# An image tower on one core: the opening rewritten so that tiles 0 to 3 share one norm and step one takes in two tiles

## What is computed

```python
h = patches(x) @ W                                   # 12544 tokens x 768 -> 256
n = layernorm(h)
x_proj = n @ in_w + in_b
mod = gelu(n @ mod_w1 + mod_b1) @ mod_w2 + mod_b2     # 256 -> 1024 -> 256
y = irfft(rfft(x_proj * mod) * rfft(kernel))          # along the 196 tokens of an image
h = h + y @ out_w + out_b
h = h + ffn(layernorm(h))                             # base, shared, and top 2 of 6 routed experts
```

## Time and profile before

| | us |
|---|---|
| three runs: median, lowest, highest | 1251.4, 1250.5, 1251.81 |
| the profiled execution | 1251.14 |
| its span, from the first to the last instruction in the trace | 1249.4 |
| TensorE busy in the span | 1226.5 (98%) |
| VectorE, ScalarE, GpSimd busy | 861.1, 587.9, 404.2 |
| TensorE's first product starts at | 7.63 |
| first projection (step one) starts at | 30.06 |
| first projection of step two starts at | 58.29 |

### The profile page before, as it was taken

The page is one execution under the profiler, slowest core; times in us unless marked ns, Lnnn a source line. Parts: engine busy times, 40 slices in busy tenths (PEclk is TensorE's granted clock), DMA queues, the critical chain, the costliest instruction groups (busy, mean ns, idle before and its releaser), DMA issues.

```text
span 1249.4 us, 21119 instructions
## 1 busy us (share of the span) xinstructions
PE 1226.5 (98%) x8163; PEld 1200.4 (96%) x8163; DVE 861.1 (69%) x2557; ACT 587.9 (47%) x1110; POOL 404.2 (32%) x463
## 2 busy tenths in 40 slices
PE   5999999999999999999999999999999999999997
PEld 5999999999999999999999999999999999999986
DVE  6467676677666677666677666677666677666676
ACT  5644454444454444454444444444444444444432
POOL 4622332322332322332322332322332322332310
PEclk9999999999999999999999999999999999999999
DMA  7111111011111011111011111011111011110001
GB/s 244 39 39 52 51 48 42 16 49 52 51 44 46 14 51 51 52 42 48 14 52 51 52 39 51 14 52 51 52 39 51 14 52 51 52 39 16 14 13 34
DMA packets 23470, 57.26 MB, mean 46 GB/s; under 512 B 2825, under 2 KB 18506, under 8 KB 19402
## 3 DMA queue, kind: packets, MB, share of 16 engines
q1 hardware_dynamic: 22554, 55.13, 12.7%
q10 hardware_dynamic: 816, 0.79, 0.2%
HBM read 43.07 MB, written 12.85 MB: 45 GB/s over the span
## 4 chain that ended last, share of the span: by engine, by line
PE 95%; DVE 3%; ACT 1%; POOL 0%; DMA 0%; issue 0%; DVEq 0%; POOLq 0%
PE rotating L1237 17%; PE rotating L1239 17%; PE rotating L1238 17%; PE rows_ps L1237 10%; PE rows_ps L1238 10%; PE rows_ps L1239 10%; PE turn L1480 5%; PE turn L1464 2%; PE turn L1276 2%; PE rows_ps L1285 2%; PE turn L1237 1%; PE turn L1238 1%; PE turn L1239 1%; PE rotating L1345 1%; POOL w_l L434 0%; DMA prod<-dram_tok_w 0%
## 5 line engine op out<-in xcount | busy, mean ns | idle before, releaser
L575 ACT ACTIVATE gelu<-rotating,biases 128x392 f32<-128x392 f32 x256 | 149.1, 583 | 203.6 <-PE rotating L1239 203.5
L468 POOL TENSOR_TENSOR folded<-modulated 128x196 f32<-128x196 f32 x63 | 38.1, 604 | 558.0 <-DVE modulated L979 558.0
L455 POOL TENSOR_TENSOR gelu_l<-gelu,gelu_h 128x784 fp32r<-128x784 f32 x62 | 117.4, 1894 | 223.4 <-DVE norm L962 197.4
L440 POOL TENSOR_TENSOR patches_l<-patches,patches_h 128x384 fp32r<-128x384 f32 x186 | 184.8, 1023 | 0.3 <-ACT patches_h L533 0.3
L1237 PE MATMUL rotating<-gelu_h,w_h 128*128 128x392 f32 x512 | 177.7, 347 | 0.0
L1237 PE MATMUL rotating<-x_h,w_h 128*128 128x392 f32 x512 | 177.2, 346 | 0.0
L1239 PE MATMUL rotating<-x_h,w_l 128*128 128x392 f32 x512 | 174.7, 341 | 0.0
L1238 PE MATMUL rotating<-x_l,w_h 128*128 128x392 f32 x512 | 174.6, 341 | 0.0
L1238 PE MATMUL rotating<-gelu_l,w_h 128*128 128x392 f32 x512 | 174.3, 340 | 0.0
L1239 PE MATMUL rotating<-gelu_h,w_l 128*128 128x392 f32 x512 | 174.0, 340 | 0.0
L1237 PE MATMUL rows_ps<-tokw_h,patches_h 128*128 128x256 f32 x576 | 165.3, 287 | 7.6 <-POOL patches_l L446 7.6
(11 more groups left out here) (259 smaller groups left out, 2922.8 us busy)
## 6 DMA issues: line engine op xcount, KB each, us to landing
patches<-dram_x_rest SPq DMA_DIRECT2D x31, 1152.0 KB, 5.1
out<-h_sb SPq DMA_DIRECT2D x30, 384.0 KB, 2.9
patches<-dram_x_first SPq DMA_DIRECT2D x3, 384.0 KB, 5.1
h_sb<-dram_x_second SPq DMA_DIRECT2D x1, 768.0 KB, 8.4
prod<-dram_tok_w ACTq DMA_DIRECT2D x2, 256.0 KB, 5.6
gelu<-dram_w SPq DMA_DIRECT2D x1, 512.0 KB, 6.7
out<-h_sb SPq DMA_DIRECT2D x1, 512.0 KB, 2.9
out<-h_sb SPq DMA_DIRECT2D x2, 256.0 KB, 2.2
```

Source lines behind the costliest of these rows:

```text
L440: pool.tensor_tensor(patches_l[:, k, :], patches[:, k, :], patches_h[:, k, :].bitcast(F32), ALU.subtract).then_inc(pool_patches_lo, 1)
L455: pool.tensor_tensor(gelu_l[:, 2 * j:2 * j + 2, :], gelu[:, 2 * j:2 * j + 2, :], gelu_h[:, 2 * j:2 * j + 2, :].bitcast(F32), ALU.subtract)\
L468: pool.tensor_tensor(folded[:, m, 0, :, 1:NF], fwd, back, ALU.add)
L575: act.activation(gelu[:, k, :], bank(g + 1, UP[k])[:, 0:GT], ACT.Gelu, bias=b1_bias[:, k:k + 1]).then_inc(act_gelu, 1)
```

## The change

- Loads: `tok_w` and the input go out in turn on SP's queue, in four pieces (k 0, k 1, k 2 and 3, k 4 and 5). Tile 5 gets a load of its own (`x_third`), tiles 6 and 7 another (`x_fourth`), and the loads behind them change places.
- TensorE starts with seven products of 512 columns on a buffer of ones, whose result nobody reads. It embeds tiles 0 to 2 as before, then tile 3, then tile 4, the latter into the banks of the next round, and tile 5 by six plain fp32 products in place of 18 (`third_tile`), two ahead of the first turn and four behind it.
- VectorE makes all low parts of tiles 0 to 4 and of `in_w`. One chain of statistics and scales serves tiles 0 to 3; ScalarE normalises two of them and VectorE two.
- GpSimd splits `w1` after that one chain. TensorE waits for `w1` only ahead of `mlp_up`, and its first projection goes by halves of the contraction (`first_project`).
- ScalarE loads the Gelu table first of all, on three zeros, and splits pieces 2 and 3 of `w2` and the input of tiles 6 and 7 within step one.
- Step one embeds two tiles in place of three, with `shared_products` ahead of them, and its norm (`stats1(2)`) is over four tiles, 4 to 7. From step two on the steps are as before.

```diff
-CHUNK = 2
+CHUNKS = ((0, 1), (1, 2), (2, 4), (4, 6))
 def intake_tiles(r):
-    return ((0, 1, 2), (3, 4))[r] if r < 2 else (3 * r - 1, 3 * r, 3 * r + 1)
+    return {0: (0, 1, 2, 3), 2: (4, 5, 6, 7)}[r] if r < 3 else (3 * r - 1, 3 * r, 3 * r + 1)
...
+            for n, (a, b) in enumerate(CHUNKS):
+                sp.dma_start(tokw_wait[n], blocks(tok_w)[:, a:b, :]).then_inc(tok_w_in[n], 16)
+                sp.dma_start(patches[:, a:b, :], x_first[:, a:b, :]).then_inc(first_in[n], 16)
...
-            first_rounds_lo()
-            split_lo("in_w")
-            pool.wait_ge(dve_ln, 2 * LN_STEPS)
-            split_lo("w1")
+            pool.wait_ge(dve_ln, LN_STEPS)
+            split_w1()
...
-            normalise(0, 0)
+            first_normalise()
+            first_x1_hi()
...
-            x1_hi(0)
-            normalise(1, 1)
-            x1_hi(1)
-            split_hi("w2")
-            patches_hi(2)
+            split_w2_hi((0,))
...
+                if i == 1:
+                    split_w2_hi((1, 2))
                 gelu_tile(mid, 0)
                 gelu_tile(mid, 1)
-                gelu_hi(mid, 0)
+                if i == 1:
+                    patches_hi(2)
+                else:
+                    gelu_hi(mid, 0)
...
-            keep_h(0)
+            split_inw()
             stats = stats1(0)
-            layer_norm_scales(0, stats, slice(0, 1), 3)
-            keep_h(1)
-            stats = stats1(1)
-            layer_norm_scales(1, stats, slice(1, 2), 2)
-            x1_lo(0)
-            x1_lo(1)
-            split_w2()
-            base_sums()
+            layer_norm_scales(0, stats, slice(0, 2), 2)
+            first_normalise()
+            keep_first_h((3, 0))
+            first_x1_lo()
+            keep_first_h((1, 2))
+            split_w2()
...
-            first_rounds()
-            pe.wait_ge(ident_in, 16)
-            spectrum_products()
-            turn_x1(0)
-            shared_products()
-            pe.wait_ge(dve_x1_lo, 1)
-            turn_x1(1)
+            ones = y_h[:, 0, 0:BANK]
+            pe.wait_ge(clock_ones, 1)
+            keep_clock(rotating[:, 2], 7, ones)
+            first_tiles()
+            second_tile(0, first_rows[3]).then_inc(pe_embed, 1)
+            second_tile(1, next_rows[0])
+            pe.wait_ge(setup_in, 16 * SETUP_LOADS)
+            spectrum_products()
+            pe.wait_ge(third_in, 16)
+            third_tile((0, 1))
+            pe.wait_ge(ident_in, 16)
+            turn_x1(0)
+            third_tile(range(2, KT)).then_inc(pe_embed, 1)
...
                 if i == 1:
+                    pe.wait_ge(dve_first_h, 4)
+                    shared_products()
+                if i == 2:
                     pe.wait_ge(base_sum, DH)
                 embed(i + 1, 0)
```

More of the change, by code:

```diff
@@ L359, in tower_program @@
         }
-        ORDER = list(splits)
-        SETUP_LOADS, CONST_LOADS = 5, 5
+        ORDER = [n for n in splits if n != "w2"]
+        LATER = ORDER[2:]
+        SETUP_LOADS, SHARED_LOADS, CONST_LOADS = 3, 2, 4
         block = ctx.enter_context(nc.Block())
@@ L494, in _ @@
                 if i == 1:
[L495 removed]
+                    for n in LATER:
                         split_lo(n)
@@ L527, in split_hi, with split_w2_hi @@
                 ins.then_inc(weight_hi, 1)
-            def patches_hi(r):
-                act.wait_ge(patches_in, 16 * (r - 1))
[L531 to L537, removed]
+            def split_w2_hi(pieces):
+                act.wait_ge(weight_in["w2"], 16 * len(splits["w2"]))
+                for n in pieces:
+                    src, waiting, hi, lo = splits["w2"][n]
+                    act.activation(hi, waiting, ACT.Copy).then_inc(w2_hi, 1)
@@ L547, in normalise, with first_x1_hi @@
                 ins.then_inc(act_norm1, 1)
+            def first_x1_hi():
+                for m in range(DH):
+                    act.wait_ge(pe_turn_x1, m + 1)
+                    act.activation(x1_h[:, m, 0:BANK], turn[:, m, :], ACT.Copy).then_inc(act_x1_hi, 1)
             def x1_hi(r):
@@ L568, in gelu_tile @@
                 act.wait_ge(pe_w1, HC * g + k + 1)
-                if g == 0 and k == 0:
-                    act.wait_ge(w2_lo, 1)
+                if g == 0 and k == 3:
+                    act.wait_ge(w2_lo, len(splits["w2"]))
                 if g > 0 and k in (0, 2):
@@ L754, in first_rounds_lo @@
                                           ALU.subtract).then_inc(dve_first_lo, 1)
-                for k in range(1, KT, 2):
+                for k in range(KT):
                     dve.wait_ge(act_patches_hi, KT + k + 1)
@@ L865, in normalise, with first_normalise, first_x1_lo @@
                 ins.then_inc(dve_norm2, 1)
+            def first_normalise():
+                dve.wait_ge(dve_ln, LN_STEPS)
+                for t in (2, 3):
+                    dve.tensor_scalar(norm1_of(0, t), first_rows[t], ln_tmp[:, 0, 1, t - 2:t - 1],
+                                      ln_tmp[:, 1, 1, t - 2:t - 1], ALU.mult, ALU.add).then_inc(dve_first_norm, 1)
+            def first_x1_lo():
+                for m in range(DH):
+                    dve.wait_ge(act_x1_hi, m + 1)
+                    dve.tensor_tensor(x1_l[:, m, 0:BANK], turn[:, m, :], x1_h[:, m, 0:BANK].bitcast(F32),
+                                      ALU.subtract).then_inc(dve_x1_lo, 1)
             def x1_lo(r):
```

295 lines of the change are left out of this document (178 added, 117 removed).

## The result

| | before | after |
|---|---|---|
| median, us | 1251.27 | 1243.86 |
| lowest to highest, us (5 runs each) | 1250.5 to 1251.81 | 1243.4 to 1245.51 |
| the profiled execution, us | 1251.14 | 1243.4 |
| first projection, step one | 30.06 | 23.04 |
| first projection, step two | 58.29 | 50.52 |

What follows compares the result with a forecast made beforehand. TensorE, 98% busy, bounds the kernel, so an earlier start of steady work counts: 7.8 + 1.6 - 1.1 - 1.0 + 2.0 - 0.9 = 8.4 us, less 0.5 for hand-offs, 7.9 earlier, median 1243.5 us; range 1241.2 to 1248.

Steps and rivals of the forecast that it cites:

- tile 3 done: Opening, TensorE's embedding: tile 3 ends at 14.9 us, between 14.5 at full pace and 15.3 if half pace lasts until 9.2.
- w1 landed, its copies done: Opening: w1 lands at 16 us and ScalarE's copies end at 18.2, hidden without slack; 1 us later costs 1 us.
- waits in mlp_up: Step one: ScalarE's longer list makes the sixth mlp_up wait 0.8 us and the seventh 0.3, 1.1 in all.
- mark: Start of step two's first projection, 58.29 us before; forecast at 50.4, 7.9 us earlier, with the end moving equally.
- The table load that went from here was hidden: ScalarE in step one: the 1.3 us table load moved to the opening had been hidden at its old place.
- the order of bytes is all that changes: Opening loads: all issuers share the same 16 full engines, so one queue only reorders bytes; 1.98 MB by 7.6 us.
- The third pair: Opening loads in one queue: the third pair of tok_w and input pieces (1.31 MB in) lands near 6.5 us.
- signs that were named for a wrong prediction: Half pace beyond 10 us, ScalarE's w1 copies ending past 19, or a wait over 2 us within step one.
- the 0.5 us added for hand-offs: About fifteen hand-offs in a row lacked latency in the counted times; 0.5 us moved the mark from 49.9 to 50.4.
- The clock came up and stayed: Rival: TensorE's clock stays at half in the opening, about 1251 or 1257 us; no gain 0.02, slower 0.03.
- The rival of late loads: Opening: tiles 0 to 2 end near the old 16.3, the norm starts 3.4 us later, 1247 us; chance 0.09.
- w2's lateness: Rival in step one: w2 lands 3 us after 21.4, ScalarE holds up mlp_up, 1246.5 us; chance 0.12.

Runs made afterwards that it cites:

- e4_w1_first: The changed kernel with all of w1's low parts waited for ahead of the first projection, as before the change: median 1245.78 us, ratio 0.9959.
- e3_late_table: The changed kernel without the early Gelu on three zeros, so the table loads ahead of step one's first real activation: median 1245.59 us, ratio 0.9955.
- e2_two_queues: The changed kernel with its four tok_w loads on ScalarE's queue again, same pieces, input on SP's: median 1246.12 us, ratio 0.9961.
- e1_no_ones: The changed kernel without its seven products on ones: median 1244.1 us, ratio 0.9945.
- e5_big_pieces: The changed kernel with three pieces of tok_w and input in place of four, all on SP's queue: median 1243.15 us, ratio 0.9936.
- b2_w1_early: The kernel before, with GpSimd's split of w1 after the first chain of scales in place of the second: median 1252.8 us, ratio 1.0013.
- f2_even_rows: `e5_big_pieces` with tok_w on ScalarE's queue and the input on SP's in loads of one block k each: median 1243.72 us, ratio 0.9939.
- g1_parts_w1: `e5_big_pieces` with w1 issued ahead of tile 5's load and step two's x1 split by halves: median 1243.38 us, ratio 0.9941.
- f3_w1_sooner: `e5_big_pieces` with w1's loads issued ahead of tile 5's load (`x_third`): median 1243.37 us, ratio 0.9936.
- b1_ones_alone: The kernel before, with only the seven products on ones added ahead of the first tiles: median 1251.18 us, ratio 0.9999.
- b3_both: The kernel before, with both the seven products on ones and w1 split after the first scales: median 1252.84 us, ratio 1.0014.

## Why the prediction was right

By its own steps, with the experiments' part in it:

| step | forecast | measured |
|---|---|---|
| full pace from | 9.2 at the latest | 6.7 |
| tile 3 done | 14.9 | 16.2 |
| scales there | 18.1 | 19.3 |
| w1 landed, its copies done | 16, 18.2 | 17.4, 19.45 |
| turn starts | 19.3 | 20.59 |
| first projection | 22.3 | 23.04 |
| waits in mlp_up (a wait of 0.43 and what follows from it) | 1.1 | 0.87 |
| shared products | 1.0 | 1.05 |
| one tile less | 2.0 | 1.92 |
| from the embedding to the mark | 10.7 | 10.50 |
| mark | 50.4 | 50.52 |

**The mechanism held.** The mark carried the whole change to the end. The earlier start, the single norm, the projection freed from w1 and the full clock gave 8.46 us up to mlp_up, and step one took back 0.69 in all. `e4_w1_first` shows that the order of projection and w1 is worth 1.7 us, `e3_late_table` that the table's move is worth 1.6 once ScalarE's list in step one is full, `e2_two_queues` that the order of the loads is worth 1.2, and `e1_no_ones` that the ones are worth 0.9 in one pair of executions. So neither the order of the bytes nor the ones did it alone: without either, the ratio is still 0.9961 and 0.9945. No run takes back the single norm or the fp32 products of tile 5 by themselves; their share is read from the timelines, not shown by an experiment. "The table load that went from here was hidden" was right for the kernel before only.

**The term that was mis-sized is the loads.** The prediction took the bytes of the kernel before, 1.98 MB by 7.6 us, and only sorted them anew; "the order of bytes is all that changes" did not hold. In the new queue 1.53 MB were there. The third pair was counted at 6.5, and its halves were used from 7.41 and 8.47, k 2 could start at 9.73 in place of 8.4, and with k 2 to 5 and tile 3 behind it (4.18 and 2.13 us, as counted) tile 3 ended 1.3 us late. w1 was late by about the same: 17.4 in place of 16. With that, one of the signs that were named for a wrong prediction came, ScalarE's w1 copies ending past 19 (19.45), and two of those for a right one did not, tile 3 near 15 and the scales near 18. `e5_big_pieces`, which changes only the pieces, gets 0.15 MB more by then and tile 3 done 0.8 us sooner, which shows that the number of loads is a cause. It is not the whole: the four small pairs bring 2.02 MB from two queues (`e2_two_queues`).

**What gave it back.** Eight turns and four fp32 products took 2.45 us in place of 2.95: the prediction took 0.47 for one such product, and the four cost 0.385 each (21.50 to 23.04). mlp_up waited 0.2 less, and the way from the embedding to the mark was 0.2 shorter. Step by step the forecast came to 49.9, which was 0.6 too early; the 0.5 us added for hand-offs, which no run shows by itself, covered that. So the loads' 1.3 us stood against errors of the other sign and an added term, and the closeness of 50.4 to 50.52 is partly luck.

**The rivals.** The clock came up and stayed, through waits of 0.37, 0.94, 0.17 and 0.43. In `b2_w1_early` it was down behind a wait of 4.44. The rival of late loads was right in its direction, a third of its size (1.2 of 3.4 us). ScalarE did hold mlp_up, once for 0.43 us, where a wait near 1 us was forecast, and w2's lateness did not show: its first piece is copied at 24.14, behind a wait of 0.82 but ahead of the x_proj copies.

**Open.** What lets two queues bring 2.02 MB by 7.6 us where one brings 1.53 wasn't settled. The number of loads alone does not decide it, since `f2_even_rows` has nine loads ahead of tiles 3 and 4, one more than the kernel after, and 1.93 MB. The time of issue may be it: one queue issued the embedding's eight loads one behind another, about 0.47 us apart, until 4.5, while before the six went out from two queues by 2.25. No run changes that by itself. And what the ones are worth in the median stays unresolved: 0.2 us between medians, 0.9 between marks.

## What to carry to other kernels

When loads are put in a new order, count the bytes again for the new number and size of loads, and don't carry the old rate over. A wait that looks idle (GpSimd's, for the second norm) can be what keeps a short chain on VectorE undisturbed; before it is lifted, look at what runs beside it. Products that raise the clock do not fix the time from which the pace is full; read it from the starts, in more than one trace, before a gain or a loss is put down to them.

## What the runs showed of the hardware

**The time of full pace varies by the execution.** With the same seven products (1.45 to 4.8), half pace lasted until 6.7 in the kernel after, 6.4 in `e4_w1_first`, at least 9.4 in `e2_two_queues`, 9.5 in `f2_even_rows`, 10.3 in `e3_late_table` and 10.4 in `g1_parts_w1`; in `e5_big_pieces` and `f3_w1_sooner` the first real products (5.86, 5.88) were at full pace. The idle time behind the seven does not sort them: 1.06 and 1.08 us in the last two named, 1.06 in `e3_late_table`, 1.02 in `g1_parts_w1`. The clock column has 1.00 in all of these stretches, and also in the trace of `b1_ones_alone`, which took 2465 us with products of 256 columns about 0.22 us apart, so the pace is to be read from the distances of starts (0.215 or 0.113 us for 256 columns), and a mark moves with it, by about 0.8 us in `g1_parts_w1`.

**Blocked, not slowed.** In `b2_w1_early` and `b3_both` three of VectorE's operations on two columns ended with GpSimd's subtractions, 0.94 to 1.19 us in place of 0.16, and the one between them (0.15) and all behind the last subtraction took their usual time.

**The same loads, another arrival.** w1 reached ScalarE at 17.45 in the kernel after, 17.69 in `e3_late_table`, 17.85 in `e1_no_ones` and 18.16 in `e4_w1_first`, with the same loads in the same order.
